# First attention of a two-attention block: its exponentials turned by VectorE and a trip through HBM instead of by TensorE

## The chip, the cores and the metric

The kernel runs on one core of a Trainium2 chip. The metric is the device time of one execution in microseconds (us). A core has five engines that run their own instruction streams and meet at semaphores: TensorE (PE; its weight loads are PEld), VectorE (DVE), ScalarE (ACT), GpSimd (POOL) and SyncE (SP), which here issues every DMA.

## What is computed

For each of 16 samples of 256 channels by 1024 positions, float32:

```python
xn = group_norm(x, 8 groups)                    # then norm_w, norm_b
q, k, v = split(qkv_w @ xn + qkv_b)             # 256 x 1024 each
x = x + proj_w @ (softmax(q.T k / 16) v.T).T + proj_b
t = tokens(x)                                   # 1024 x 256
u = layer_norm(t);  n = u / |u|
t = t + softmax((n n.T) ** 2) u
y = sign(w - mean(w)) * mean(|w|) applied to layer_norm(t), + bias
t = t + round(7 * clip(y, -1, 1)) / 7
out = tokens back to channels
```

Both softmaxes are over rows of 1024. Products are made of float32 values cut into a high and a low float32r part, three matmuls in the place of one (low x high, high x low, high x high), so each operand of a product exists twice, as `_hi` and `_lo`.

## The kernel before

One sample follows the other, software-pipelined by hand: `front(b, f)` does the first attention of sample b and the scores of the second, together with the feed-forward layer of the sample before (f = b - 1), and `back(b)` does the eight products of the second attention. The order of every engine's work is written out by hand in its block's `front` and `back`, and 14 of the 16 samples run in a hardware loop.

The first attention goes in eight blocks n of 128 queries. `scores1(b, n)` (PE, L405) writes 128 x 1024 scores into PSUM `wide[n % 2]`, `row_max` (DVE, L889) takes the negative maximum of each row, `exp1` (ACT, L665) writes the exponentials to `expo` in SBUF together with the row sums. The product with v needs the exponentials with keys on the partitions, so `turn_e1` (PE, L429) turns the block by eight 128 x 128 transposes into PSUM `turn`; `e1T_hi` (ACT, L672) rounds it to `eT_hi`, `e1T_lo` (DVE, L894) writes the rest to `eT_lo`, and `product1` (PE, L437) multiplies with v in 24 matmuls of 256 columns. `turn_e1` of block s stands right before `product1` of block s - 1. `residual1` (DVE, L898) divides by the row sum, adds x and takes the moments of the row; POOL makes the coefficients of the layer norm (`layer_norm1`, L1116) and the inverse length of the row (`lengths`, L1119), ACT the normed rows (L678), POOL the unit rows (`unit_rows`, L1132), PE turns these (`turn_cos`, L447), and `cosT_hi`/`cosT_lo` (ACT, DVE) write `tokT_hi` and `tokT_lo`.

The second attention's scores (`scores2`, L455) are computed for the lower triangle alone, in nine parts of growing width; `exp2` (ACT, L698) squares and exponentiates, `e2_hi` (DVE, L916) and `e2_lo` (POOL, L1146) cut the parts, `turn_e2` (PE, L474) and `e2T_parts` (DVE, L927) make the mirrored half. The feed-forward part is `turn_ln2` (PE), `ln2T_hi` (ACT), `ln2T_lo` (DVE), `ffn` (PE, L515), `ffn_out` (ACT), `clip` (DVE), `quantise` (POOL), `turn_t` (PE) and `output` (DVE). `gn_sums`, `group_means`, `gn_deviation`, `group_vars`, `gn_variance` belong to the next sample's group norm.

## Time and profile before

| | us |
|---|---|
| three runs, median | 1856.28 (1855.66 to 1859.16) |
| the profiled execution's own time | 1856.45 |
| its span | 1854.7 |
| TensorE busy | 1835.7 (99%) |
| VectorE, GpSimd, ScalarE busy | 1268.1 (68%), 959.6 (52%), 906.7 (49%) |
| DMA, mean over the span | 19 GB/s |

The span is the time from the first to the last instruction in the profile; 1.75 us lie around it. TensorE's granted clock is 0.998 of full speed on average.

### The profile page before, as it was taken

The numbers are of one execution on the slowest core, as the hardware profiler recorded it, in microseconds if no ns is written. First come the engines' busy times: TensorE is split into PE (matmuls) and PEld (weight loads), VectorE is DVE, ScalarE is ACT, GpSimd is POOL, SyncE is SP. The second block draws the span as 40 slices with busy tenths as digits, with TensorE's granted clock in tenths as the row PEclk, the third lists the DMA queues.
The fourth block names the chain that finished last, engine by engine and source line by source line (L and its number), as shares of the span: only waits on it lengthen the run. The fifth ranks groups of instructions, "written<-read, shape, count | busy, mean of one in ns | idle before, by whom it ended". The sixth has DMA issues, their size and how long they took to land.

```text
span 1854.7 us, 36871 instructions
## 1 busy us (share of the span) xinstructions
PE 1835.7 (99%) x12834; PEld 1699.1 (92%) x12834; DVE 1268.1 (68%) x2516; ACT 906.7 (49%) x1444; POOL 959.6 (52%) x2262
## 2 busy tenths in 40 slices
PE   7999999999999999999999999999999999999997
PEld 6999999989899998999989999999998999989997
DVE  6676766767666676666767667676676766767566
ACT  3545546445463544635446354454544536355452
POOL 0654727457274472734737356372654727447272
PEclk9999999999999999999999999999999999999999
DMA  2000010000100001000010100001000010000000
GB/s 77 1 24 24 1 45 0 23 23 0 45 0 23 23 0 45 0 34 11 0 45 0 45 0 10 35 0 45 0 23 23 0 45 0 23 23 0 24 1 23
DMA packets 16415, 35.42 MB, mean 19 GB/s; under 512 B 2688, under 2 KB 4096, under 8 KB 16384
## 3 DMA queue, kind: packets, MB, share of 16 engines
q1 hardware_dynamic: 16384, 35.01, 5.2%
q8 instruction: 19, 0.31, 0.1%
q14 instruction: 12, 0.10, 0.0%
HBM read 18.23 MB, written 16.78 MB: 19 GB/s over the span
## 4 chain that ended last, share of the span: by engine, by line
PE 98%; DVE 0%; DMA 0%; ACT 0%; SPq 0%; issue 0%; POOL 0%; ACTq 0%; POOLq 0%; DVEq 0%
PE wide L322 35%; PE narrow L424 8%; PE narrow L426 8%; PE narrow L425 8%; PE turn L434 6%; PE wide L424 5%; PE wide L426 5%; PE wide L425 5%; PE narrow L322 5%; PE wide L520 3%; PE turn L481 3%; PE turn L377 2%; PE narrow L452 2%; PE turn L511 1%; PE turn L528 1%; DMA qkv_b_c<-in_L_conv_qkv_b 0%
## 5 line engine op out<-in xcount | busy, mean ns | idle before, releaser
L322 PE MATMUL wide<-xn_hi,prob 128*128 128x512 f32 x1024 | 310.1, 404 | 0.0
L676 ACT ACTIVATE prob<-turn 128x1024 fp32r<-128x1024 f32 x128 | 131.3, 1026 | 322.0 <-PE turn L434 322.0
L1109 POOL TENSOR_TENSOR ln_v<-ln_mv,ln_eps 128x1 f32<-128x1 f32 x256 | 49.3, 193 | 428.8 <-DVE ln_mv L909 251.7
L891 DVE TENSOR_REDUCE neg_max<-wide 128x1 f32<-128x1024 f32 x128 | 156.4, 1222 | 123.0 <-PE wide L322 123.0
L690 ACT ACTIVATE ln<-tok,ln_shift,ln_r 128x256 f32<-128x256 f32 x128 | 77.2, 603 | 319.7 <-POOL ln_shift L1114 319.7
L424 PE MATMUL narrow<-prob 128*128 128x256 f32 x768 | 225.0, 293 | 0.0
L426 PE MATMUL narrow<-prob 128*128 128x256 f32 x768 | 217.0, 283 | 0.0
L425 PE MATMUL narrow<-prob 128*128 128x256 f32 x768 | 216.9, 282 | 0.0
L322 PEld LDWEIGHTS wide<-xn_hi,prob 128*128 128x128 f32 x1024 | 182.8, 188 | 35.4
L896 DVE TENSOR_TENSOR prob<-turn,prob 128x1024 fp32r<-128x1024 f32 x128 | 156.7, 1224 | 61.8 <-ACT prob L676 61.8
L669 ACT ACTIVATE expo<-wide,neg_max 128x1024 f32<-128x1024 f32 x128 | 142.5, 1113 | 58.2 <-DVE neg_max L891 58.1
L322 PE MATMUL wide<-xn_lo,prob 128*128 128x512 f32 x512 | 160.7, 395 | 0.0
L1149 POOL TENSOR_TENSOR prob<-expo,prob 128x128 fp32r<-128x128 f32 (+6 forms) x112 | 150.3, 1358 | 9.0 <-DVE prob L919 9.0
L424 PE MATMUL narrow<-val,prob 128*128 128x258 f32 x512 | 148.6, 290 | 0.0
L425 PEld LDWEIGHTS narrow<-prob 128*128 128x128 f32 x768 | 147.1, 191 | 0.0
L424 PE MATMUL wide<-val,prob 128*128 128x258 f32 x512 | 146.9, 287 | 0.0
L424 PEld LDWEIGHTS narrow<-prob 128*128 128x128 f32 x768 | 146.9, 191 | 0.0
L426 PEld LDWEIGHTS narrow<-prob 128*128 128x128 f32 x768 | 146.7, 191 | 0.0
L1138 POOL TENSOR_TENSOR cos_x<-ln_x,len_i 128x256 f32<-128x256 f32 x128 | 78.7, 615 | 130.7 <-ACT ln_x L683 126.6
L426 PE MATMUL wide<-val,prob 128*128 128x258 f32 x512 | 145.0, 283 | 0.0
L426 PE MATMUL narrow<-val,prob 128*128 128x258 f32 x512 | 145.0, 283 | 0.0
L425 PE MATMUL wide<-val,prob 128*128 128x256 f32 x512 | 144.6, 282 | 0.0
(171 smaller groups left out, 5479.1 us busy)
## 6 DMA issues: line engine op xcount, KB each, us to landing
x_raw<-in_x SPq DMA_DIRECT2D x32, 512.0 KB, 3.9
out<-y_sb SPq DMA_DIRECT2D x32, 512.0 KB, 2.8
tok<-in_L_conv_qkv_w SPq DMA_DIRECT2D x1, 768.0 KB, 6.8
ln<-in_L_conv_proj_w SPq DMA_DIRECT2D x1, 256.0 KB, 6.8
ln<-in_L_ffn_weight SPq DMA_DIRECT2D x1, 256.0 KB, 3.0
out_bias<-in_L_conv_proj_b SPq DMA_DIRECT2D x1, 128.0 KB, 3.8
qkv_b_c<-in_L_conv_qkv_b SPq DMA_DIRECT2D x1, 3.0 KB, 7.4
norm_w_c<-in_L_conv_norm_w SPq DMA_DIRECT2D x1, 1.0 KB, 6.1
```

What stands on the lines that cost most here:

```text
L322: mm = pe.matmul(o, lhsT, r, start=first and i == 0, stop=last and i == len(parts) - 1)
L424: pe.matmul(o[:, 0:w], hi, value_hi(j), start=j == 0, stop=False)
L425: pe.matmul(o[:, 0:C], hi, value_lo(j), start=False, stop=False, skip_group_check=True)
L426: mm = pe.matmul(o[:, 0:w], lo, value_hi(j), start=False, stop=j == NT - 1)
L434: mm = pe.transpose(turn[:, tile(j)], expo[:, n % DEEP, tile(j)], ident[:, :])
L669: act.activation(expo[:, n % DEEP], wide[n % 2][:, :], ACT.Exp, bias=neg_max[:, n:n + 1], accum_out=row_sum1[:, n:n + 1]).then_inc(e1_made, 1)
L676: act.activation(eT_hi[:, n % 2], turn[:, :], ACT.Copy).then_inc(eT_hi_made, 1)
L690: act.activation(ln2[:, n], tok[:, n], ACT.Identity, bias=ln2_shift[:, n:n + 1], scale=ln2_r[:, n:n + 1]).then_inc(ln2_made, 1)
L891: dve.tensor_reduce(neg_max[:, n:n + 1], wide[n % 2][:, :], AX.X, ALU.max, negate=True).then_inc(max_made, 1)
L896: dve.tensor_sub(eT_lo[:, n % 2], turn[:, :], eT_hi[:, n % 2].bitcast(F32)).then_inc(eT_made, 1)
L1138: pool.tensor_tensor(cos_x[:, r], ln_x[:, r], len_i[:, n:n + 1].broadcast_to([P, C]), ALU.mult).then_inc(cos_made, 1)
L1149: pool.tensor_sub(prob[:, 1, J, row], expo[:, J % DEEP, row], prob[:, 0, J, row].bitcast(F32)).then_inc(p_made, 1)
```

## The change

The eight TensorE transposes of a block of the first attention are taken out. In their place VectorE turns each 32 x 32 square of the block in itself (`e1_turn`), from `expo` into `e_turned` (which is the memory of `x_norm`), SyncE writes the block to a scratch tensor in HBM (`send`, one DMA of 512 KB) and reads it back with the squares at their turned places (`fetch`, four DMAs of 32 partitions, 128 KB each, in runs of 1 KB) into `e_back`. From there `e1T_hi` (ACT) and `e1T_lo` read; `e1T_lo` is on POOL for blocks 0 to 3 and on DVE for 4 to 7. `product1(n)` moves from one block behind the scores to four behind at first: the scores start earlier, between the feed-forward steps of the sample before. Because `x_norm` is lent to the trip, `normalise` moves from the middle of `front` to `back` on ACT. The feed-forward results move from `wide` to `turn`. The row work of the layer norms is grouped: `GROUPS1` cuts the eight blocks into (0,1), (2,3), (4,5), (6), (7) for the first, and three groups serve the second, with one set of POOL coefficient instructions for a group; `unit_rows` goes from POOL to ACT, one instruction per block.

```diff
         a_hi = prob[:, 0, 0:KC, :]
         a_lo = prob[:, 0, KC:2 * KC, :]
         v = prob[:, 0, 2 * KC:2 * KC + NT // 2, :].rearrange("p a (t c) -> p (a t) c", t=2)
-        eT_hi = prob[:, 1, 0:2, :]
-        eT_lo = prob[:, 1, 2:4, :]
+        eT_hi = prob[:, 1, 4:6, :]
+        eT_lo = prob[:, 1, 6:8, :]
+        e_turned = x_norm
+        e_back = sb("e_back", [P, 2, SQ, NT * Q])
+        e_scratch = nc.dram_tensor("e_scratch", (NT, P, N), F32).ap()
+        e_in = e_scratch.rearrange("n (i j) (q f) -> n q j i f", i=SQ, q=SQ)
...
-        out1 = [narrow[0]] * (NT - 2) + [wide[0][:, BANK:N], wide[1][:, BANK:N]]
+        out1 = [narrow[0]] * 4 + [turn[:, 0:BANK], narrow[0], wide[0][:, BANK:N], wide[1][:, BANK:N]]
+        gn_up = turn[:, BANK:BANK + KC]
...
                 load_x(b)
 
+            def send(b, n):
+                sp.wait_ge(e1_turned, NT * b + n + 1)
+                sp.dma_start(e_scratch[n], e_turned[:, n % 2]).then_inc(e1_written[n % 2], 16)
+
+            def fetch(b, n):
+                due = 16 * (HT * b + n // 2 + 1)
+                sp.wait_ge(e1_written[n % 2], due)
+                sp.wait_ge(eT_made[n % 2], due)
+                for q in range(SQ):
+                    sp.dma_start(e_back[q * Q:(q + 1) * Q, n % 2], e_in[n, q]).then_inc(e1_landed[n % 2], 16)
+
+            def front(b, f):
+                send(b, 0)
+                send(b, 1)
+                fetch(b, 0)
+                send(b, 2)
+                fetch(b, 1)
+                send(b, 3)
+                fetch(b, 2)
+                send(b, 4)
...
-            def turn_e1(b, n):
-                pe.wait_ge(e1_made, NT * b + n + 1)
-                if n:
-                    pe.wait_ge(eT_made, NT * b + n)
-                for j in range(NT):
-                    mm = pe.transpose(turn[:, tile(j)], expo[:, n % DEEP, tile(j)], ident[:, :])
-                mm.then_inc(eT_up, 1)
...
             def product1(b, n):
                 if n == 0:
                     pe.wait_ge(v_made, 4 * b + 4)
-                elif n < NT - 2:
+                elif n < 4:
                     pe.wait_ge(t1_made, NT * b + n)
-                pe.wait_ge(eT_made, NT * b + n + 1)
+                elif n == 5:
+                    pe.wait_ge(t1_made, NT * b + 4)
+                pe.wait_ge(eT_made[n % 2], 16 * (HT * b + n // 2 + 2))
                 mm = product(out1[n], lambda j: (eT_hi[:, n % 2, tile(j)], eT_lo[:, n % 2, tile(j)]),
                              lambda j: v[:, j, 0:C], lambda j: v[:, j, C:2 * C])
                 mm.then_inc(pv1_up, 1)
...
+                scores1(b, 0)
+                if f is not None:
+                    pe.wait_ge(xT_made, 2 * b + 2)
+                    turn_ln2(f, 0)
+                scores1(b, 1)
                 values(b, 2)
                 values(b, 3)
                 if f is not None:
-                    pe.wait_ge(a_made, 2 * b + 2)
+                    ffn(f, 0)
+                scores1(b, 2)
+                if f is not None:
+                    pe.wait_ge(y_made, 4 * f + 2)
+                    turn_ln2(f, 1)
+                scores1(b, 3)
+                if f is not None:
                     ffn(f, 1)
+                scores1(b, 4)
+                if f is not None:
+                    pe.wait_ge(y_made, 4 * f + 4)
                     turn_t(f, 0)
-                    pe.wait_ge(y_made, 4 * f + 2)
-                scores1(b, 0)
+                product1(b, 0)
+                scores1(b, 5)
                 if f is not None:
                     pe.wait_ge(out_made, 2 * f + 1)
                     turn_t(f, 1)
-                    pe.wait_ge(y_made, 4 * f + 4)
-                scores1(b, 1)
+                product1(b, 1)
+                scores1(b, 6)
+                product1(b, 2)
...
+                if more:
+                    group_means(b + 1)
+                scores1(b, 7)
+                turn_cos(b, 0)
+                if more:
+                    group_vars(b + 1)
+                product1(b, 3)
+                scores2(b, 0)
+                scores2(b, 1)
+                product1(b, 4)
+                product1(b, 5)
+                turn_cos(b, 1)
+                product1(b, 6)
...
+                    pe.wait_ge(gn_var, b + 2)
+                turn_e2(b, 1)
+                scores2(b, 2)
+                scores2(b, 3)
+                turn_cos(b, 2)
+                product1(b, 7)
+                turn_e2(b, 2)
+                scores2(b, 4)
+                turn_e2(b, 3)
+                turn_cos(b, 3)
+                scores2(b, 5)
+                turn_e2(b, 4)
+                scores2(b, 6)
+                turn_e2(b, 5)
+                turn_cos(b, 4)
+                scores2(b, 7)
+                scores2(b, 8)
+                turn_e2(b, 6)
...
             def e1T_hi(b, n):
-                act.wait_ge(eT_up, NT * b + n + 1)
+                act.wait_ge(e1_landed[n % 2], 16 * SQ * (HT * b + n // 2 + 1))
                 if n >= 2:
                     act.wait_ge(pv1_up, NT * b + n - 1)
-                act.activation(eT_hi[:, n % 2], turn[:, :], ACT.Copy).then_inc(eT_hi_made, 1)
...
+                e1T_hi(b, 0)
+                exp1(b, 3)
+                if f is not None:
                     ffn_out(f, 1, reuse)
...
+                e1T_hi(b, 1)
+                exp1(b, 4)
+                e1T_hi(b, 2)
+                exp1(b, 5)
+                e1T_hi(b, 3)
+                layer_norm1(b, 0)
+                exp1(b, 6)
+                unit_rows(b, 0)
+                e1T_hi(b, 4)
+                exp1(b, 7)
+                cosT_hi(b, 0)
...
+                layer_norm1(b, 2)
+                exp2(b, 2)
+                unit_rows(b, 2)
+                exp2(b, 3)
+                cosT_hi(b, 2)
+                layer_norm1(b, 3)
+                unit_rows(b, 3)
+                exp2(b, 4)
+                cosT_hi(b, 3)
+                layer_norm1(b, 4)
+                unit_rows(b, 4)
+                exp2(b, 5)
+                exp2(b, 6)
+                cosT_hi(b, 4)
+                exp2(b, 7)
+                exp2(b, 8)
...
+            def e1_turn(b, n):
+                dve.wait_ge(e1_made, NT * b + n + 1)
+                if n >= 2:
+                    dve.wait_ge(e1_written[n % 2], 16 * (HT * b + n // 2))
+                dve.transpose(e_turned[:, n % 2].rearrange("p (q n t) -> p n q t", q=SQ, n=NT),
+                              expo[:, n % DEEP].rearrange("p (n q t) -> p n q t", q=SQ, n=NT)).then_inc(e1_turned, 1)
+
             def e1T_lo(b, n):
                 dve.wait_ge(eT_hi_made, NT * b + n + 1)
-                dve.tensor_sub(eT_lo[:, n % 2], turn[:, :], eT_hi[:, n % 2].bitcast(F32)).then_inc(eT_made, 1)
+                dve.tensor_sub(eT_lo[:, n % 2].rearrange("p (n i t) -> p n i t", n=NT, i=SQ),
+                               e_back[:, n % 2].rearrange("p i (n t) -> p n i t", n=NT),
+                               eT_hi[:, n % 2].rearrange("p (n i t) -> p n i t", n=NT, i=SQ).bitcast(F32)
+                               ).then_inc(eT_made[n % 2], 16)
...
+                row_max(b, 6)
+                e1_turn(b, 6)
+                residual1(b, 2)
+                if more:
+                    gn_deviation(b + 1)
+                e1T_lo(b, 4)
+                row_max(b, 7)
+                cosT_lo(b, 0)
+                e1_turn(b, 7)
+                if more:
+                    gn_variance(b + 1)
+                residual1(b, 3)
+                e1T_lo(b, 5)
+                e2_hi(b, 0)
...
+                residual1(b, 7)
+                e2T_parts(b, 2)
+                e2_hi(b, 4)
+                cosT_lo(b, 3)
+                e2T_parts(b, 3)
+                e2_hi(b, 5)
+                e2T_parts(b, 4)
+                cosT_lo(b, 4)
+                e2_hi(b, 6)
+                e2T_parts(b, 5)
+                e2_hi(b, 7)
+                e2_last_lo(b, 7)
+                e2T_parts(b, 6)
+                e2_hi(b, 8)
+                e2_last_lo(b, 8)
...
+            def e1T_lo(b, n):
+                pool.wait_ge(eT_hi_made, NT * b + n + 1)
+                pool.tensor_sub(eT_lo[:, n % 2].rearrange("p (n i t) -> p n i t", n=NT, i=SQ),
+                                e_back[:, n % 2].rearrange("p i (n t) -> p n i t", n=NT),
+                                eT_hi[:, n % 2].rearrange("p (n i t) -> p n i t", n=NT, i=SQ).bitcast(F32)
+                                ).then_inc(eT_made[n % 2], 16)
...
             def front(b, f, more):
                 if f is not None:
                     quantise(f, 0)
+                e1T_lo(b, 0)
+                e1T_lo(b, 1)
+                if f is not None:
                     quantise(f, 1)
-                for n in range(NT - 1):
-                    layer_norm1(b, n)
-                    lengths(b, n)
-                    unit_rows(b, n)
-                    value_lo(b, n)
```

The functions `layer_norm1`, `lengths`, `value_lo`, `turn_cos`, `cosT_hi` and `cosT_lo` take a group g in the place of a block n and work on all of its blocks.

**Where the order moves, first place.** ScalarE, from the first feed-forward output to the second exponential blocks, before (`tokT_hi<-turn` is `ln2T_hi`, `y_sb` is `ffn_out`, `prob<-narrow` is `value_hi`, `expo,row_sum1` is `exp1`, `prob<-turn` is `e1T_hi`):

```order
L712 ACTIVATE tokT_hi<-turn 128x2x512 [waits ln2T_up]
L721 ACTIVATE y_sb<-wide0,ffn_b_c,w_mean 128x512 [waits y_up]
L721 ACTIVATE y_sb<-wide0,ffn_b_c,w_mean 128x512
L661 ACTIVATE prob<-narrow0 128x2x256 [waits v_up]
L661 ACTIVATE prob<-narrow1 128x2x256 [waits v_up]
L721 ACTIVATE y_sb<-wide1,ffn_b_c,w_mean 128x512 [waits y_up]
L721 ACTIVATE y_sb<-wide1,ffn_b_c,w_mean 128x512
L669 ACTIVATE expo,row_sum1<-wide0,neg_max 128x1024 [waits max_made]
L676 ACTIVATE prob<-turn 128x1024 [waits eT_up]
L669 ACTIVATE expo,row_sum1<-wide1,neg_max 128x1024 [waits max_made]
L676 ACTIVATE prob<-turn 128x1024 [waits eT_up]
```

and now, from the same feed-forward output:

```order
L796 ACTIVATE y_sb<-turn,ffn_b_c,w_mean 128x512 [waits y_up]
L796 ACTIVATE y_sb<-turn,ffn_b_c,w_mean 128x512
L727 ACTIVATE expo,row_sum1<-wide0,neg_max 128x1024 [waits max_made]
L787 ACTIVATE tokT_hi<-turn 128x2x512 [waits ln2T_up]
L734 ACTIVATE prob<-e_back 128x1024 [waits e1_landed0]
L727 ACTIVATE expo,row_sum1<-wide1,neg_max 128x1024 [waits max_made]
L796 ACTIVATE y_sb<-turn,ffn_b_c,w_mean 128x512 [waits y_up]
L796 ACTIVATE y_sb<-turn,ffn_b_c,w_mean 128x512
```

The second `ln2T_hi` stood ahead of the first feed-forward output and of all exponentials; now it stands behind the third exponential, and the second `ffn_out` behind the fourth.

**Second place.** ScalarE around the last exponential of the first attention, before (`ln_x` and `val` are `layer_norm1`, `x_norm` is `normalise`, `tokT_hi<-narrow1` is `cosT_hi`):

```order
L645 ACTIVATE x_norm<-x_raw,gn_b,gn_a 128x1024 [waits gn_scale]
L695 ACTIVATE tokT_hi<-narrow1 128x2x128 [waits cosT_up]
L676 ACTIVATE prob<-turn 128x1024 [waits pv1_up,eT_up]
L669 ACTIVATE expo,row_sum1<-wide1,neg_max 128x1024 [waits eT_up,max_made]
L683 ACTIVATE ln_x<-tok,ln_shift,ln_r 128x256 [waits val_made,ln1_scale]
L686 ACTIVATE val<-ln_x 128x256 [waits ln1_made]
L695 ACTIVATE tokT_hi<-narrow1 128x2x128 [waits cosT_up]
L676 ACTIVATE prob<-turn 128x1024 [waits pv1_up,eT_up]
```

and now (`cos_x` is `unit_rows`, `prob<-e_back` is `e1T_hi`):

```order
L727 ACTIVATE expo,row_sum1<-wide0,neg_max 128x1024 [waits e1_turned,max_made]
L756 ACTIVATE cos_x<-ln_x,len_i 128x256 [waits len_steps]
L756 ACTIVATE cos_x<-ln_x,len_i 128x256
L734 ACTIVATE prob<-e_back 128x1024 [waits pv1_up,e1_landed0]
L727 ACTIVATE expo,row_sum1<-wide1,neg_max 128x1024 [waits e1_turned,max_made]
L768 ACTIVATE tokT_hi<-narrow1 128x2x256 [waits cosT_up]
L734 ACTIVATE prob<-e_back 128x1024 [waits pv1_up,e1_landed1]
```

Three `cosT_hi` of a sample stood ahead of its last exponential (the third is the second row shown); now the first of them is the instruction right behind that exponential.

**Third place.** VectorE in the second attention, before (`prob<-expo` is `e2_hi`, `prob<-turn` is `e2T_parts`, `tokT_lo` is `cosT_lo`):

```order
L919 CAST prob<-expo 128x512 [waits e2_made]
L930 CAST prob<-turn 128x3x128 [waits pT_up]
L932 TENSOR_TENSOR prob<-turn,prob 128x3x128 [waits pT_hi_made]
L913 TENSOR_TENSOR tokT_lo<-narrow1,tokT_hi 128x2x128 [waits cosT_hi_made]
L919 CAST prob<-expo 128x640 [waits e2_made]
L930 CAST prob<-turn 128x4x128 [waits pT_up]
L932 TENSOR_TENSOR prob<-turn,prob 128x4x128 [waits pT_hi_made]
L919 CAST prob<-expo 128x768 [waits e2_made]
L913 TENSOR_TENSOR tokT_lo<-narrow1,tokT_hi 128x2x128 [waits cosT_hi_made]
L930 CAST prob<-turn 128x5x128 [waits pT_up]
L932 TENSOR_TENSOR prob<-turn,prob 128x5x128 [waits pT_hi_made]
L919 CAST prob<-expo 128x896 [waits e2_made]
```

and now:

```order
L1023 CAST prob<-expo 128x640 [waits e2_made]
L1017 TENSOR_TENSOR tokT_lo<-narrow1,tokT_hi 128x2x128 [waits cosT_hi_made]
L1034 CAST prob<-turn 128x3x128 [waits pT_up]
L1036 TENSOR_TENSOR prob<-turn,prob 128x3x128 [waits pT_hi_made]
L1023 CAST prob<-expo 128x768 [waits e2_made]
L1034 CAST prob<-turn 128x4x128 [waits pT_up]
L1036 TENSOR_TENSOR prob<-turn,prob 128x4x128 [waits pT_hi_made]
L1017 TENSOR_TENSOR tokT_lo<-narrow1,tokT_hi 128x2x128 [waits cosT_hi_made]
L1023 CAST prob<-expo 128x896 [waits e2_made]
L1034 CAST prob<-turn 128x5x128 [waits pT_up]
```

The turned halves of block 4 (`128x4x128`) stood ahead of the cast of block 5 (`128x768`); now they stand behind it. The last `cosT_lo` stood ahead of the halves of block 5 and now too, but it belongs to a `turn_cos` that TensorE issues right before the scores that need it.

## Rows read from the trace of the kernel before

**Rows 1.** Page, part 1: busy us (share) xinstructions

```profile
PE 1835.7 (99%) x12834; PEld 1699.1 (92%) x12834; DVE 1268.1 (68%) x2516; ACT 906.7 (49%) x1444; POOL 959.6 (52%) x2262
```

**Rows 2.** TensorE's waits: who waited for whom, us, times, longest

```profile
PE narrow L364 <- DVE gn_mv L856: 7.3, 1, 7.3
```

**Rows 3.** Chain of waits in order of time: start us, us, what

```profile
949.80 0.87 PE turn L434 x8
...
954.36 0.12 PE narrow L424
...
957.23 2.81 PE wide L322 x12
...
1000.84 1.39 PE wide L322 x6
...
1006.88 0.44 PE turn L481 x4
...
1007.54 2.47 PE wide L322 x12
```

**Rows 4.** Groups by line: busy us, mean ns | idle before

```profile
L896 DVE TENSOR_TENSOR prob<-turn,prob 128x1024 fp32r<-128x1024 f32 x128 | 156.7, 1224 | 61.8 <-ACT prob L676 61.8
...
L712 ACT ACTIVATE tokT_hi<-turn 128x1024 fp32r<-128x1024 f32 x31 | 31.7, 1021 | 33.0 <-PE turn L511 33.0
...
L695 ACT ACTIVATE tokT_hi<-narrow 128x256 fp32r<-128x256 f32 x128 | 47.9, 374 | 18.0 <-PE narrow L452 16.9
...
L913 DVE TENSOR_TENSOR tokT_lo<-narrow,tokT_hi 128x256 fp32r<-128x256 f32 x128 | 52.5, 410 | 21.9 <-ACT tokT_hi L695 21.9
...
L683 ACT ACTIVATE ln_x<-tok,ln_shift,ln_r 128x256 f32<-128x256 f32 x128 | 76.6, 599 | 10.5 <-POOL ln_shift L1114 10.5
```

**Rows 5.** Timeline, one sample of the loop: start us, us, engine, line, operation

```profile
945.96 1.03 PE L528 MATMUL turn<-ident,tok 128*128 128x128 f32 x8
...
946.16 1.23 DVE L891 TENSOR_REDUCE neg_max<-wide 128x1 f32<-128x1024 f32 x1 [0.36 <-PE wide L322]
...
947.42 1.12 ACT L669 ACTIVATE expo<-wide,neg_max 128x1024 f32<-128x1024 f32 x1 [3.48 <-DVE neg_max L891]
...
948.43 0.19 ACT L669 ACTIVATION_READ_ACCUMULATOR expo<-wide,neg_max 128x1 f32 x1
```

**Rows 6.** Timeline, VectorE between the score blocks

```profile
963.94 0.16 DVE L861 COPY gn_m<-narrow 128x2 f32<-128x2 f32 x1 [0.71 <-PE narrow L364]
...
965.06 0.16 DVE L867 TENSOR_TENSOR gn_e<-gn_e,gn_mv 128x2 f32<-128x2 f32 x1
...
984.30 0.17 DVE L902 RECIPROCAL inv_sum<-row_sum 128x1 f32<-128x1 f32 x1 [0.58 <-PE narrow L426]
...
985.51 0.06 DVE L804 MEMSET carrier<- 128x1 f32 x1
```

**Rows 7.** Timeline, ScalarE and VectorE in the second attention

```profile
1007.05 0.81 ACT L706 ACTIVATE expo<-wide 128x768 f32<-128x768 f32 x1 [0.50 <-PE wide L322]
...
1007.49 0.68 DVE L930 CAST prob<-turn 128x512 fp32r<-128x512 f32 x1
...
1007.90 0.85 ACT L708 ACTIVATE expo<-expo 128x768 f32<-128x768 f32 x1
...
1008.81 0.93 DVE L919 CAST prob<-expo 128x768 fp32r<-128x768 f32 x1
```

**Rows 8.** Groups by line, GpSimd and VectorE

```profile
L1104 POOL TENSOR_TENSOR xn_lo<-x_norm,xn_hi 128x1024 fp32r<-128x1024 f32 x30 | 80.7, 2709 | 0.0
...
L924 DVE TENSOR_TENSOR prob<-expo,prob 128x512 fp32r<-128x512 f32 x32 | 82.1, 2567 | 1.1
```

**Rows 9.** Page, part 6: DMA issues, KB each, us to landing

```profile
x_raw<-in_x SPq DMA_DIRECT2D x32, 512.0 KB, 3.9
...
out<-y_sb SPq DMA_DIRECT2D x32, 512.0 KB, 2.8
```

**Rows 10.** Windows at the end: us, busy of each engine, PEclk, DMA

```profile
1845.00:1850.00 5.00, 3.06 (x12) 2.36 (x10) 3.02 (x4) 1.45 (x2) 0.00 (x0) 0.72 0.27 105
```

More of the change, by code:

```diff
@@ L36 @@
 BANK = 512
+Q = 32
 GROUPS = 8
@@ L731, in front @@
                 if f is not None:
-                    ln2T_hi(f, 1)
-                    ffn_out(f, 0, reuse)
+                    ln2T_hi(f, 0)
+                exp1(b, 0)
+                exp1(b, 1)
                 value_hi(b, 2)
@@ L755, in front @@
-                cosT_hi(b, 5)
-                for u in range(2, NP):
-                    J = PARTS[u][0]
-                    if J in (4, 6):
-                        cosT_hi(b, J // 2 + 4)
-                    exp2(b, u)
-                    if J == 3:
-                        layer_norm1(b, NT - 1)
+                    ffn_out(f, 0, reuse)
+                exp1(b, 2)
+                if f is not None:
+                    ln2T_hi(f, 1)
+                e1T_hi(b, 0)
+                exp1(b, 3)
@@ L984, in front @@
                 value_lo(b, 1)
+                row_max(b, 0)
+                if f is not None:
+                    ln2T_lo(f, 0)
+                e1_turn(b, 0)
+                row_max(b, 1)
+                value_lo(b, 2)
+                e1_turn(b, 1)
+                value_lo(b, 3)
+                if f is not None:
+                    clip(f, 0)
+                row_max(b, 2)
                 if f is not None:
                     ln2T_lo(f, 1)
-                    clip(f, 0)
-                value_lo(b, 2)
@@ L989, in front @@
-                value_lo(b, 3)
+                e1_turn(b, 2)
+                row_max(b, 3)
+                e1_turn(b, 3)
                 if f is not None:
                     clip(f, 1)
+                row_max(b, 4)
+                if f is not None:
                     output(f, 0)
-                row_max(b, 0)
+                e1_turn(b, 4)
+                residual1(b, 0)
+                if more:
+                    gn_sums(b + 1, 0)
+                row_max(b, 5)
                 if f is not None:
@@ L995, in front @@
                     output(f, 1)
-                row_max(b, 1)
-                e1T_lo(b, 0)
+                e1_turn(b, 5)
+                residual1(b, 1)
                 if more:
-                    gn_sums(b + 1, 0)
-                for s in range(1, NT + 1):
-                    if more and s == 3:
-                        gn_deviation(b + 1)
-                    if s >= 2:
-                        residual1(b, s - 2)
-                    if s + 1 < NT:
-                        row_max(b, s + 1)
-                    if more and s == 3:
-                        gn_variance(b + 1)
-                    if s >= 4:
-                        cosT_lo(b, s - 4)
-                    if s < NT:
-                        e1T_lo(b, s)
-                    if more and s == 1:
-                        gn_sums(b + 1, 1)
@@ L1015, in front @@
[L1015 to L1029 removed]
+                    gn_sums(b + 1, 1)
@@ new lines, in front @@
+                e1T_lo(b, 6)
+                residual1(b, 5)
+                cosT_lo(b, 1)
+                e1T_lo(b, 7)
+                residual1(b, 6)
+                e2T_parts(b, 1)
+                e2_hi(b, 2)
+                e2_hi(b, 3)
+                cosT_lo(b, 2)
+                residual1(b, 7)
[5 more added lines that the diff above has]
+                e2T_parts(b, 4)
```

339 lines of the change are left out of this document (170 added, 169 removed).

## The prediction

> **What bounds the kernel now.** I read the busy times first: TensorE works 1835.7 of 1854.7 us, the others half to two thirds of the span [rows 1]. Then its waits: the longest is 7.3 us, once, at the start [rows 2]; in the loop there are none. So each microsecond taken from TensorE is one taken from the time, as long as nobody makes it wait in its place. The chain in order of time is TensorE's program and gives serial prices [rows 3]: the eight transposes of `turn_e1` 0.87 us, a `scores1` 2.81, a `product1` 2.87 (954.36 to 957.23), the scores of part 3 1.39, of part 6 2.47, `turn_e2(4)` 0.44.
>
> **What goes.** 16 samples x 8 blocks x 0.87 = 111.4 us. The profiled execution took 1856.45 us (span 1854.7 and 1.75 around it; the median of the three runs is 1856.28), so without one new wait the time would be 1745.1. The break-even is 111.4 / 16 = 6.96 us of TensorE waiting per sample.
>
> **Where TensorE would wait.** The other engines work in order, so what counts is where each row stands in its queue. I walked through one sample with prices from rows: a row-wide tensor operation on DVE 1.22 [rows 4], a `row_max` 1.23 and, 0.2 behind the end of a TensorE group; `exp1` 1.12 and 0.19 for its sums, 1.20 until the next engine may start; a hand-over between DVE and ACT 0.03 [rows 5]. The VectorE turn is nowhere in this trace. It moves 1024 elements per partition, as the rows at 1.22 do, so 1.22 is the nearest and what I take; below, 0.7 as for 512 columns [rows 7], if two elements moved at a time; above, twice the row, 2.45.
>
> A. `ffn(1)` behind `scores1(3)`. The second `ln2T_hi` now stands behind `exp1(2)` on ACT (first place of the order). From the end of `scores1(2)`: 0.20 + 1.23 + 0.03 + 1.12 + 1.02 [rows 4] + 1.22 for `ln2T_lo` = 4.8. TensorE has `turn_ln2(1)` and `scores1(3)` in that time, 0.87 + 2.81 = 3.7. Wait 1.15.
>
> B. `turn_t(0)` wants the second `ffn_out`, which stands behind `exp1(3)`; DVE comes to that row's maximum only after `ln2T_lo` and `e1_turn(2)`. Wait 0.2.
>
> C. `group_vars` wants `gn_deviation`. On DVE it stands behind `e1_turn(6)` (1.22) and `residual1(2)` (984.30 to 985.57: 1.3), and takes 1.3 itself (963.94 to 965.22) [rows 6]; the turn can't start before `exp1(6)`, which on ACT stands behind the first pair of layer norms and ends about 0.35 after `product1(2)`. That makes 0.35 + 3.7 = 4.05 from the product's end; TensorE comes there at 0.12 + 2.81 + 0.4 = 3.35. Wait 0.7.
>
> D. `scores2(0)` wants the first `cosT_lo`. Ahead of it stand `e1T_lo(4)`, `row_max(7)`, `exp1(7)` and `cosT_hi(0)` (second place). From the same product's end: `row_max(7)` starts at 5.2, then 1.23 + 1.20 + 0.6 + 0.7 for the two halves of 512 columns (they lie between the 256 and the 1024 columns of [rows 4]), 9.0. TensorE, C included, is there at 4.1 + 0.1 + 2.87 = 7.1. Wait 1.7 to 1.9; I take 1.7. Were DVE free for `row_max(7)` at once, 0.5 would stay.
>
> E. `turn_cos(1)` behind `product1(5)`: its unit rows stand on ACT behind the layer norms of blocks 2, 3 and `e1T_hi(6)`, all of it hanging on `residual1(3)`, which D has made late. 0.7, and 0.2 more before `product1(6)`. 0.9.
>
> F. `turn_cos(2)` behind `scores2(3)`: from the end of part 2, 0.2 + two passes over 384 columns, 1.05, + two scalings of 256 columns, 1.1 [rows 4] = 2.35; TensorE has 1.39. Wait 0.95.
>
> G. `turn_e2(5)` wants the turned halves of block 4, which now stand behind the cast of block 5 (third place). From the end of `scores2(5)`: ACT is free at 0.7 (a layer norm and its unit row stand first), then 0.81 + 0.85, cast 0.93, halves 0.68 and 0.7 [rows 7] = 4.7. TensorE has 0.44 + 2.47 = 2.9. Wait 1.75; with ACT free and the cast at 0.5, 0.9.
>
> H. `turn_cos(4)` stands right before the `scores2(7)` that needs it: 0.2 + 0.37 + 0.41 [rows 4] after the transposes. Wait 1.0. Before, a block of scores lay between.
>
> The sum is 1.15 + 0.2 + 0.7 + 1.7 + 0.9 + 0.95 + 1.75 + 1.0 = 8.35 us per sample, x 16 = 133.6. The first sample has no feed-forward part and so neither A nor B, but its `product1(0)` comes so soon behind the scores that it waits some 3 us for the trip; I count it like the others. 1745.1 + 133.6 = 1878.7, so **1879 us**.
>
> **What is hidden.** The trip: a store of 512 KB lands in 2.8 us, a load in 3.9 [rows 9]; four issues for one make it some 4.4, so 7.2 both ways. By my walk (us from the sample's start): `fetch(n)` is queued on SP behind `send(n + 1)` or further, so block 0, turned at 17.5 us of the sample, is back at 27.2, rounded at 28.7, its low part at 31.4 (2.7 on POOL [rows 8]), and `product1(0)` starts at 34.7: 3.3 to spare. Blocks 1, 2, 3 have 2.4, 2.8, 2.3. With ACT in order, a trip longer by 2 us would first hold up `exp1(3)` and `exp1(4)`. Blocks 5 and 6 have 0.7 and nothing. The ACT and POOL instructions that were regrouped stand beside TensorE's work; POOL loses the unit rows, and ACT's eight scalings of 0.6 are in E, F and G. `normalise` in `back` has 24 us of `product2` over it.
>
> A row speaks against `e1T_lo`: a DVE subtraction of 512 columns with both inputs in SBUF, while POOL works, takes 2.57 us, where 1024 columns with one input in PSUM take 1.22 [rows 8, 4]. The new `e1T_lo` has both in SBUF, on DVE for blocks 4 to 7, with POOL busy. Between 1.22 and 1.22 + 2.7 (a whole POOL subtraction first); I take 1.22 but for block 6, where 0.5 more is in E. At its worst blocks 5 and 6 come 2.7 late, 2 us per sample beyond their slack, and the time is 1878.7 + 32 = 1911. The Trainium skill (SBUF — State Buffer, "Who interferes with whom") says that a VectorE instruction with two SBUF inputs and a GpSimd one that uses SBUF exclude each other for a whole instruction; by that rule the 1911 would be the sum, by the row of 1.22 it is 1879.
>
> **Rivals.**
> 1. *The side engines keep up, and the change is faster.* For: they idle a third to half of the time [rows 1], and B, C, E hang on queues in which I may have put an instruction too early. Against: A, F, G, H are chains within the sample that start at TensorE itself. With B, C, E at nothing, D 0.5, G 0.9: 4.5 per sample, 1745.1 + 72 = 1817; halfway 1840. The change is faster from under 6.96 us of waits per sample on.
> 2. *The turn takes twice a pass, 2.45.* B, C (and D behind it) and E each grow by 1.2: 3.6 x 16 = 58, 1937. Against: nothing in the trace.
> 3. *Products wait*, for the ports (above) or for the trip: 1 to 2 us in two products per sample, 1911 to 1940.
> 4. *The clock falls.* At the end of this trace TensorE works 3.06 of 5 us with some 1.9 of idle time between, and its granted clock there is 0.72 of full speed, from 1.0 [rows 10]: that is its 2.4 GHz level left for its 1.2 GHz level part of the time. G and H leave it 0.7 us of work in 3.5. If the 3.4 us of matmuls behind them ran at 1.2 GHz, that is 3.4 x 16 = 55 more, 1934. Against: none of my gaps is as long as that one. The Trainium skill (TensorE: Matmul & The Clock Gate, "Part 1: The HAM clock gate") calls this a gate that an idle engine closes; by it this rival would hold if G and H count as idle, and else not.
>
> **How the numbers follow.** Forecast (waits of 7.2 to 10 per sample, 1860 to 1905) 0.45; rival 1 0.30; rival 2 0.08; rival 3 0.09; rival 4 0.08. A measurement of this kernel tells 0.2% (3.7 us) from no change. Within it lie waits of 6.7 to 7.2 per sample, an edge of the forecast and of rival 1: 0.05. Faster 0.28, slower 0.67. The forecast's own range is 1860 to 1905; the range that leaves out 2 in 10 goes from rival 1's floor, 1818, to above rivals 2 and 4, 1942.
>
> **What would show it.** In the changed profile: `turn_e1` gone and TensorE's busy time near 1725 us; its waits, by total: `ffn` <- `ln2T_lo`, `scores2` <- `cosT_lo` (D and H), `turn_cos` <- unit rows of ACT, `turn_e2` <- `e2T_parts`, each once or twice per sample and 16 to 28 us in all; the turn at 1.2 us; no product's wait over 0.5 us per sample; PEclk 1.0. Wrong it would be if `turn_e2` and `turn_cos` don't wait, if the turn costs 2 us, or if a DMA stands in TensorE's or ACT's longest waits.

## The result, and the profile after

The changed kernel takes 1975.79 us (median of four, 1972.13 to 1978.41) against 1855.97 for the kernel before: a ratio of 1.0641, 95% interval 1.0628 to 1.0654. It is 6.4% slower. The direction was forecast; the size was not, and 1976 lies 34 us above the range's end of 1942. Two single executions of the experiments lie far outside all others (1993 us for the kernel before, beside x5 to x8, and 3584 us for x8) and are left out of their ratios.

The page of the changed kernel, first the line that answers to [rows 1], then the granted clock in 40 slices (tenths of full speed; before all 40 were 9, the highest digit there is):

```profile
PE 1811.1 (92%) x11810; PEld 1638.6 (83%) x11810; DVE 1267.9 (64%) x2532; ACT 936.5 (47%) x1476; POOL 880.2 (45%) x1398
...
PEclk9999999999999989999999999989999899998999
```

TensorE has 1024 instructions less, as it should, but its busy time fell by 24.6 us and not by 111. So there are two losses: waits, and work that got longer. The waits of TensorE (who waited for whom: us, times, longest), against the one line of [rows 2]:

```profile
PE turn L525 <- DVE prob L1036: 39.2, 16, 2.5
PE wide L368 <- DVE tokT_lo L1017: 38.1, 32, 1.6
PE narrow L495 <- ACT cos_x L756: 24.3, 26, 1.6
PE turn L415 <- DVE gn_e L959: 16.6, 16, 1.3
PE turn L564 <- DVE tokT_lo L1054: 15.8, 15, 1.1
PE wide L470 <- DVE prob L995: 9.0, 16, 0.7
PE turn L410 <- DVE gn_mv L948: 7.2, 1, 7.2
PE narrow L470 <- POOL prob L1237: 3.1, 1, 3.1
```

These are G, D with H, E with F, C and A of the prediction, and the wait of `product1(6)`; the two that occur once belong to the first sample. All waits of the list come to 158.7 us; before they came to 12.3. That is 146.4 more.

The second loss. Windows of the changed kernel, from one sample (us; busy and count of PE, PEld, DVE, ACT, POOL; granted clock; DMA share; GB/s):

```profile
1044.00:1048.00 4.00, 2.55 (x22) 2.35 (x21) 2.24 (x3) 2.64 (x4) 0.00 (x0) 1.00 0.49 166
1048.00:1052.00 4.00, 4.00 (x23) 4.00 (x23) 3.15 (x10) 1.39 (x4) 3.14 (x7) 0.57 0.83 260
...
1076.00:1080.00 4.00, 1.67 (x9) 1.34 (x10) 2.40 (x5) 1.34 (x3) 1.94 (x2) 0.90 0.00 0
1080.00:1084.00 4.00, 4.00 (x15) 3.16 (x14) 1.64 (x3) 1.35 (x3) 1.97 (x1) 0.67 0.00 0
```

Twice per sample TensorE is back at work, busy all the time, at a granted clock near half: its 1.2 GHz level in place of 2.4. The timeline of TensorE around both places shows which waits stand ahead (start, us, what; in brackets the idle time before and who ended it):

```profile
1042.64 0.38 PE L415 MATMUL turn<-gn_e,group_mean 128*128 128x2 f32 x2 [0.90 <-DVE gn_e L959]
...
1047.45 0.32 PE L368 MATMUL wide<-tokT_hi,tokT_lo 128*128 128x128 f32 x1 [1.45 <-DVE tokT_lo L1017]
...
1049.28 0.41 PE L470 MATMUL turn<-prob 128*128 128x256 f32 x1
...
1052.11 0.28 PE L472 MATMUL turn<-prob 128*128 128x256 f32 x1
```

```profile
1077.40 0.76 PE L525 MATMUL turn<-ident,expo 128*128 128x128 f32 x5 [2.47 <-DVE prob L1036]
1077.99 0.38 PE L495 MATMUL narrow<-ident,cos_x 128*128 128x128 f32 x2
1079.31 0.80 PE L368 MATMUL wide<-tokT_hi,tokT_lo 128*128 128x512 f32 x1 [0.93 <-DVE tokT_lo L1017]
1079.90 0.63 PE L368 MATMUL wide<-tokT_lo,tokT_hi 128*128 128x512 f32 x1
```

A `product1` matmul takes 0.41 us behind the first pair of waits (C and D) and 0.28 three microseconds later; a score matmul over 512 columns takes 0.63 behind the second pair (G and H), and 0.40 elsewhere. No wait of these four is longer than 2.5 us.

This sample doesn't stand for all. In 15 samples the second fall stands behind G and H. The first stands behind C and D in 6 of them only; in the other 9 the clock holds there and falls some 10 us later, behind the two waits of E (`turn_cos(1)` and `product1(6)`). One of the nine:

```profile
560.06 0.32 PE L368 MATMUL wide<-tokT_hi,tokT_lo 128*128 128x128 f32 x1 [1.45 <-DVE tokT_lo L1017]
560.22 0.28 PE L368 MATMUL wide<-tokT_lo,tokT_hi 128*128 128x128 f32 x1
...
568.54 0.63 PE L495 MATMUL narrow<-ident,cos_x 128*128 128x128 f32 x4 [1.08 <-ACT cos_x L756]
569.82 0.39 PE L470 MATMUL wide<-prob 128*128 128x256 f32 x1 [0.65 <-DVE prob L995]
...
571.08 0.41 PE L472 MATMUL wide<-prob 128*128 128x256 f32 x1
```

Over the span, in windows of 2 us, the granted clock is down at 33 places, each of which costs up to 1.7 or 3.4 us; before there were 2, both at the end of the program. The mean granted clock is 0.962; before it was 0.998. Of 1976.3 us that takes at most (1 - 0.962) x 1976.3 = 75 us, before it took at most 4. TensorE was busy in 135 of the 150 us at the lower level, which makes 68.

The book then nearly closes: 1854.7 - 111.4 + 146.4 + 71 = 1960.7, and the span is 1976.3. The 16 left (21 with the 68) would be 0.13 us for each of the 121 waits that are new. That they belong to the waits isn't shown by a run of its own; the rows above show only that the first matmul behind a wait takes 0.32 to 0.39 us, where later ones of the kind take 0.28 and overlap, one every 0.12 us.

### The profile page after: what moved, and what is told of

It reads as the page before. It is cut to its first block, busy times and chain, and to the rows that moved or that the text cites. A ratio compares the mean times of both kernels' runs of the same rounds, so it can differ in the third digit from the quotient of the medians.

```text
span 1976.3 us, 34635 instructions
## 1 busy us (share of the span) xinstructions
PE 1811.1 (92%) x11810; PEld 1638.6 (83%) x11810; DVE 1267.9 (64%) x2532; ACT 936.5 (47%) x1476; POOL 880.2 (45%) x1398
## 4 chain that ended last, share of the span: by engine, by line
PE 46%; POOL 23%; issue 14%; DVE 5%; ACT 5%; DMA 3%; SPq 2%; POOLq 1%; ACTq 0%; DVEq 0%
PE wide L368 16%; POOL prob L1237 5%; PE narrow L368 4%; PE wide L470 3%; PE wide L472 3%; PE wide L471 3%; PE narrow L470 3%; PE narrow L472 3%; PE narrow L471 3%; DMA e_back<-e_scratch 3%; POOL val L1276 3%; POOL ln_r L1250 2%; POOL sq_root L1264 2%; PE turn L525 2%; POOL prob L1282 2%
## 5 line engine op out<-in xcount | busy, mean ns | idle before, releaser
L1237 POOL TENSOR_TENSOR prob<-e_back,prob 128x1024 fp32r<-128x1024 f32 x64 | 153.5, 2399 | 162.4 <-ACT prob L734 161.3
L990 DVE STREAM_TRANSPOSE x_norm<-expo 128x1024 f32<-128x1024 f32 x128 | 158.7, 1240 | 79.0 <-ACT expo L727 77.0
L470 PE MATMUL narrow<-prob 128*128 128x256 f32 x640 | 185.8, 290 | 3.1 <-POOL prob L1237 3.1
L471 PE MATMUL narrow<-prob 128*128 128x256 f32 x640 | 182.0, 284 | 0.0
L472 PE MATMUL narrow<-prob 128*128 128x256 f32 x640 | 181.9, 284 | 0.0
L1282 POOL TENSOR_TENSOR prob<-expo,prob 128x128 fp32r<-128x128 f32 (+6 forms) x112 | 159.5, 1424 | 46.6 <-DVE prob L1023 46.6
L734 ACT ACTIVATE prob<-e_back 128x1024 fp32r<-128x1024 f32 x128 | 135.0, 1055 | 78.9 <-DMA e_back<-e_scratch 78.3
L368 PE MATMUL wide<-tokT_hi,tokT_lo 128*128 128x512 f32 (+3 forms) x384 | 137.2, 398 | 38.1 <-DVE tokT_lo L1017 38.1
L1247 POOL TENSOR_TENSOR ln_v<-ln_mv,ln_eps 128x2 f32<-128x2 f32 (+2 forms) x128 | 26.7, 208 | 318.4 <-DVE ln_mv L1049 244.8
L781 ACT ACTIVATE expo<-wide 128x128 f32<-128x128 f32 (+2 forms) x144 | 85.3, 593 | 142.4 <-PE wide L368 140.9
L1292 POOL TENSOR_TENSOR carrier_p<-ones 128x1 f32<-128x1 f32 x60 | 11.7, 195 | 316.0 <-DVE y_sb L1059 313.5
L1023 DVE CAST prob<-expo 128x128 fp32r<-128x128 f32 (+2 forms) x144 | 80.4, 567 | 111.0 <-ACT expo L783 111.0
```

The source lines that it names most:

```text
L368: mm = pe.matmul(o, lhsT, r, start=first and i == 0, stop=last and i == len(parts) - 1)
L470: pe.matmul(o[:, 0:w], hi, value_hi(j), start=j == 0, stop=False)
L471: pe.matmul(o[:, 0:C], hi, value_lo(j), start=False, stop=False, skip_group_check=True)
L472: mm = pe.matmul(o[:, 0:w], lo, value_hi(j), start=False, stop=j == NT - 1)
L734: act.activation(eT_hi[:, n % 2].rearrange("p (n i t) -> p n i t", n=NT, i=SQ), e_back[:, n % 2].rearrange("p i (n t) -> p n i t", n=NT), ...
L781: act.activation(e, wide[J % 2][:, offset(J) + c0:offset(J) + c1], ACT.Square).then_inc(sq2_made, 1)
```

## The experiments

Two theories went into them. A: the loss is the waits at the places that the walk named, plus a clock that falls behind gaps close together. B: the longer matmuls have another cause (the DMA traffic, the SBUF rows). Later a third, C: the waits aren't the order's, and move on when one is taken away. All runs stand beside runs of the kernel before (1855.8 to 1857.0). "Rest" is the span, less waits, less unread matmuls, less the 1731.0 that before has without waits (1842.4) and without the transposes (111.4).

| run | us (median) | waits | clock | falls | (1 - clock) x span | rest |
|---|---|---|---|---|---|---|
| changed kernel | 1975.8 | 158.7 | 0.962 | 33 | 75 | 87 |
| x1 fillers, 40 | 1993.1 | 128.4 | 0.983 | 18 | 34 | 47 |
| x5 fillers, 24 | 1933.9 | 80.9 | 0.996 | 3 | 8 | 20 |
| x2 swap at G | 1922.4 | 137.4 | 0.984 | 18 | 31 | 49 |
| x3 swap at D | 1944.9 | 156.2 | 0.981 | 17 | 37 | 53 |
| x4 five places | 1890.8 | 114.6 | 0.988 | 11 | 23 | 42 |
| x6 x4 and three more | 1878.1 | 103.2 | 0.987 | 13 | 24 | 40 |
| x8 x6 and fillers, 7 | 1860.2 | 78.3 | 0.997 | 3 | 6 | 18 |
| x9 x6 and three others | 1893.1 | 121.3 | 0.991 | 10 | 17 | 38 |
| x10 x9 and fillers, 2 | 1893.2 | 110.6 | 0.988 | 13 | 23 | 38 |
| x11 x9, GpSimd's order | 1897.4 | 113.3 | 0.983 | 17 | 32 | 49 |
| x12 x11 without G's swap | 1929.3 | 141.4 | 0.974 | 19 | 50 | 55 |
| x7 turn at 2.45 | 2077.6 | 233.7 | 0.953 | 42 | 98 | 116 |

All but the first column are of the profiled execution. The clock's column is an upper bound, as TensorE is idle in part of the time at the lower level. The rest follows it in every row, 5 to 21 us above it.

**Fillers.** They make nothing earlier. In x5, beside x1 (the waits that keep these PSUM parts free are left out):

```
+def busy(o, n):
+    for _ in range(n):
+        pe.matmul(o, sign_w[:, 0, 0:P], sign_w[:, :, :], start=True, stop=True)
 product1(b, 3)
+busy(wide[0][:, 0:BANK], 5)       # x1: 10 of 256 columns
 scores2(b, 0)
...
 product1(b, 5)
+busy(wide[0][:, BANK:N], 4)       # x1: none
 turn_cos(b, 1)
...
+busy(narrow[0][:, :], 3)          # x1: 6 of 256
 turn_cos(b, 2)
...
 scores2(b, 6)
+busy(narrow[0][:, :], 9)          # x1: 18 of 256
 turn_e2(b, 5)
 turn_cos(b, 4)
+busy(narrow[0][:, :], 3)          # x1: 6 of 256
 scores2(b, 7)
```

x1: 

> The changed kernel with small matmuls that nobody reads (128x256, 0.12 us apart) put where TensorE waits: 10 before scores2(0), 18 before turn_e2(5), 6 before turn_cos(2), 6 before scores2(7). They are shorter than or as long as the waits there, so no wait goes and nothing gets earlier. Theory A (the gaps make the granted clock fall, and the work behind them at the lower level is what my sum lacked): granted clock back to 0.99 or more, the slow matmuls behind the gaps gone, 1976 - 60 to 80 = 1895 to 1915 us. Rival B (the longer matmuls come from something else, the DMA trip or the two-input VectorE rows): clock and time as they are, 1976 or, where a filler is longer than its wait, up to 1985.

Measured 1993.1 us, clock 0.983. Wrong in the sum, but 15 of the 33 falls were gone. Two things ate it: the falls that are left (9 behind `turn_cos(1)`, which had no filler, and 6 beside the stall), and a stall at the head of the loop that stands in no other kernel's list of TensorE's waits. The first line of x1's:

```profile
PE narrow L470 <- issue: 36.8, 12, 4.0
```

x5: 

> As the first filler kernel, but with 24 unread matmuls of 512 columns (0.23 us apart) in place of 40 of 256: 5 before scores2(0), 4 before turn_cos(1), 3 before turn_cos(2), 9 before turn_e2(5), 3 before scores2(7). The first one removed the clock falls behind scores2(0) and turn_e2(5), but had a new one behind turn_cos(1) and a stall of 2 to 4 us without a releaser at the head of the loop. Theory A: with turn_cos(1) filled too no fall is left, the clock is 0.99 or more, and without that stall 1976 - 70 = 1895 to 1915 us; with the stall (12 times some 3 us) 1935 to 1950. Rival B (the lower clock isn't the gaps' doing): no change, or more.

Measured 1933.9 us, clock 0.996: 42 us faster than the changed kernel, with 384 matmuls more. The stall did not come back. The unread matmuls were busy for 102.9 us while the waits gave up 77.8, so they cost 25, and the rest fell from 87 to 20. That is the cause shown: with the gaps filled, and every other engine's program as it was, 67 us go. Theory B can't do that.

**One swap each.**

```
# x2, VectorE
 e2T_parts(b, 3)
-e2_hi(b, 5)
 e2T_parts(b, 4)
+e2_hi(b, 5)
# x3, ScalarE
+cosT_hi(b, 0)
 exp1(b, 7)
-cosT_hi(b, 0)
```

x2: 

> The changed kernel with one pair swapped on VectorE: the turned halves of block 4 (e2T_parts) ahead of the cast of block 5. Theory A: the wait of turn_e2(5) goes (2.45 us, 16 times: 39 us) and with it the second clock fall of a sample (1.7 us lost, 27 us): 1976 - 66 = 1910. Without the clock in it: 1937. Rival C (the wait is not the order's, it turns up one step later): above 1960.

Measured 1922.4: 53 us gained. The wait went (39.2 to 0) and 15 falls with it, but the wait behind `cosT_lo` grew from 38.1 to 56.4 us: TensorE now comes to H sooner than the `cosT_lo` that it needs, and waits 2.09 us there in place of 0.93.

x3: 

> The changed kernel with one pair swapped on ScalarE: the first cosT_hi ahead of exp1(7). Theory A: the wait of scores2(0) goes (about 1.45 us x 16 = 23) and with it the first clock fall of a sample (27 us), as the gap of 0.9 at group_vars then stands alone: 1976 - 50 = 1926. Without the clock: 1953. Rival C (scores2(0) then waits for exp1(7) or a low part just the same): above 1965.

Measured 1944.9: 31 us gained. D's wait went (38.1 to 14.9, which is H's) and 16 falls, and `turn_cos` waits 42.0 in place of 24.3. Of the first falls of a sample only three are left, at E, and none stands behind C, which waits 1.1 us alone now. Both swaps pay less than forecast (66 and 50 us) but more than the waits they remove (21 and 3 us in the sum of all waits): the rest goes with the clock's column (44 and 38 us less).

**All five places** (D, G; H: `turn_cos(4)` ahead of `turn_e2(5)` and `cosT_hi(4)` ahead of the third `exp2` from the end; A: second `ln2T_hi` ahead of `exp1(2)`; C: `group_means` and `gn_deviation` ahead of `product1(2)` and `residual1(2)`).

x4: 

> The changed kernel with five places of the orders altered: e2T_parts(4) ahead of the cast of block 5, first cosT_hi ahead of exp1(7), turn_cos(4) ahead of turn_e2(5) and its cosT_hi ahead of exp2(6), second ln2T_hi ahead of exp1(2), group_means and gn_deviation ahead of product1(2) and residual1(2). Theory A: waits A, C, D, G, H of the prediction (16 + 17 + 23 + 39 + 15 = 110 us) and both clock falls go; left are turn_cos behind unit rows (24), the products' low parts (12) and the start (10): 1745 + 46 = 1790 to 1810, faster than before. Rival C (the side engines have no slack, waits move on): 1860 to 1930.

Measured 1890.8 us: 85 us gained where 165 to 185 were expected, so theory C holds for half of it. A is gone from the list, C became a wait of the same size at `group_means`, and D's gain turned up at `turn_cos(1)`, whose unit rows wait for GpSimd. Behind its wait of 1.77 us and the product's of 0.63 stand 8 of the 11 falls that are left.

**Three more:** `group_means` back, `residual1(3)` ahead of `e1_turn(7)` on VectorE, `gn_coefficients` behind the second `lengths` on GpSimd.

x6: 

> The order kernel before with three more edits: group_means back behind product1(2) with only gn_deviation ahead of residual1(2); residual1(3) ahead of e1_turn(7) on VectorE; gn_coefficients behind the second group's lengths on GpSimd. Theory A: the waits at group_means (19 us) and at turn_cos(1) (1.77 x 16 = 28, to under 10) go, and with the latter the last clock fall (27 us); 1890 - 19 - 20 - 27 = 1825 us, faster than before. Rival C (the side engines have no slack, waits move on): 1860 to 1890.

Measured 1878.1 us. The wait of `turn_cos(1)` went from 1.77 us to nothing, and that of `turn_cos(2)` grew to 2.85, with the clock's fall behind it in ten samples of sixteen (windows of x6, one of the ten):

```profile
1006.00:1010.00 4.00, 1.15 (x8) 0.74 (x7) 2.29 (x7) 3.90 (x9) 3.75 (x8) 1.00 0.00 0
1010.00:1014.00 4.00, 4.00 (x23) 4.00 (x22) 1.12 (x2) 2.35 (x5) 3.61 (x9) 0.57 0.00 0
```

x8 (four unread matmuls ahead of `turn_cos(1)` and three ahead of `turn_cos(2)`): 

> The order kernel with the three more edits and seven unread matmuls of 512 columns per sample, 4 before turn_cos(1) and 3 before turn_cos(2). Theory A: if the edits alone leave a clock fall behind these two places, this takes it away: 15 to 30 us under the kernel without fillers. If they leave none: the same, or up to 10 us slower, as the fillers are then longer than the waits.

Measured 1860.2 us, ratio to the kernel before 1.0019 (1.0009 to 1.0030). Seven matmuls that compute nothing make it 18 us faster. It is the best of all the versions and still no faster than the kernel before.

**What GpSimd makes late.**

x9 (`unit_rows(2)` ahead of `exp2(2)`; the coefficients and lengths of blocks 4 and 5 ahead of `value_lo(1)`, `e2_lo(1)` and `gn_coefficients`; `gn_deviation` ahead of `e1_turn(6)`): 

> The order kernel with the three more edits (1878 us, of which turn_cos(2) waits 2.85 us once a sample, 42 us in all, and one clock fall stands behind it), and three edits that shorten what turn_cos(2) and group_vars wait for: on GpSimd the second-group low parts and gn_coefficients behind the lengths of blocks 4 and 5, on ScalarE unit_rows(2) ahead of exp2(2), on VectorE gn_deviation ahead of e1_turn(6). Theory A: the wait of turn_cos(2) falls from 2.85 to 0.8 us (33 us) and the clock fall goes (some 27 us), group_vars saves 10: 1878 - 70 = 1808 us, clock 0.99 or more, faster than before. Rival C (waits move on): 1850 to 1878. The floor is 1745 plus what is left of waits.

x10 (x9 and two fillers): 

> The same with two unread matmuls of 512 columns ahead of turn_cos(2). Theory A: no clock fall is left to take away, so this costs nothing to 8 us (32 x 0.23); if a fall is still there, 20 us less than without them.

x11 (x9 with `gn_deviation` back, and block 6's coefficients and lengths ahead of `e2_lo(1)` too): 

> The order kernel with the three more edits (1878 us), unit_rows(2) ahead of exp2(2) on ScalarE, and on GpSimd the coefficients and lengths of blocks 4 and 5 and then of block 6 ahead of e2_lo(1), the low parts of group 2 and gn_coefficients; gn_deviation stays behind e1_turn(6). In the kernel of 1893 us product1(3) waited 1.38 us behind that deviation and turn_cos(3) 1.46 us, as GpSimd came to block 6 4.6 us after its rows. Theory A: both go, and the chain behind turn_cos(3) (exp2(5), turn_e2(5), scores2(7)) gets earlier: 1893 - 10 - 23 - 15 = 1845 us, clock 0.99 or more, faster than before. Rival C (waits move on): 1870 to 1890.

Measured 1893.1, 1893.2 and 1897.4, each 15 to 19 us slower than x6. The sums of x9 and x11 are wrong, each beyond its rival's range too. x10's fillers cost nothing, as its theory A said, but not for its reason: falls were left, 10 in x9 and 13 in x10. In both kernels most of them stand behind `scores2(7)`, where x10 has no filler. In x9 `turn_cos(2)` waits 0.79 in place of 2.85, and the 2 us come back as 1.38 at `product1(3)`, 1.46 at `turn_cos(3)` and 1.23 at `scores2(7)`. In x11 (timeline, TensorE) the chain behind `turn_cos(4)`, H's edit, stands bare:

```profile
1029.89 0.41 PE L495 MATMUL narrow<-ident,cos_x 128*128 128x128 f32 x2 [1.13 <-ACT cos_x L756]
...
1031.37 0.77 PE L525 MATMUL turn<-ident,expo 128*128 128x128 f32 x5 [1.07 <-ACT expo L783]
...
1033.34 0.79 PE L368 MATMUL wide<-tokT_hi,tokT_lo 128*128 128x512 f32 x1 [1.20 <-DVE tokT_lo L1017]
```

From a block's residual to its unit rows it takes four and five tiny GpSimd operations in a row, 4.5 us (x6: 994.55 to 999.0), and this chain runs four times between the last score block and `product2`. My reading is that with the transposes gone there is less of TensorE's work to lie over the chain than it is long, and that a wait ahead of it had hidden its later parts. It is read from these three traces and not shown: no run shortened the chain.

**One gap in a kernel of short ones.**

x12: 

> The kernel run beside it, with the one pair on VectorE (cast of block 5, turned halves of block 4) back in the order of the changed kernel, so that turn_e2(5) waits about 2.5 us again, the other waits being short. If one gap of 2.5 us is enough for a clock fall: 2.5 + some 1.7 us per sample, 60 to 70 us over the kernel beside it, clock about 0.985. If the falls need gaps close together: 40 us, clock as beside it.

Measured 1929.3 us, 32 over x11, clock 0.974 against 0.983. Neither case: x11 has a fall of its own at this place in nearly every sample (three gaps of 1.1 to 1.2 us close together), and in x12 the gap is 4.10 us, not 2.5; the clock falls inside it, while TensorE does nothing (windows of x12):

```profile
1044.00:1048.00 4.00, 1.65 (x8) 0.96 (x7) 0.17 (x1) 3.07 (x7) 3.77 (x7) 1.00 0.00 0
1048.00:1052.00 4.00, 1.13 (x6) 1.13 (x7) 3.76 (x5) 1.83 (x3) 2.94 (x3) 0.62 0.00 0
1052.00:1056.00 4.00, 4.00 (x11) 3.13 (x11) 1.65 (x2) 1.04 (x2) 1.98 (x1) 0.52 0.00 0
```

**The dearer turn.** An unread reduction of 1.2 us ahead of each turn on VectorE:

```
+dve.tensor_reduce(unread[:, n:n + 1], expo[:, n % DEEP], AX.X, ALU.max)
 dve.transpose(e_turned[:, n % 2]..., expo[:, n % DEEP]...)
```

x7: 

> The changed kernel with an unread row-wide reduction (1.2 us) on VectorE ahead of each e1_turn, so that the turn costs 2.45 us as rival 2 of the prediction supposed. By the walk of the prediction waits B, C, D and E grow by 1.2 each: 3.6 to 4.8 us per sample, 1976 + 58 to 77 = 2034 to 2053; with the clock falling longer behind them up to 2080. If VectorE had slack in this stretch: under 2000.

Measured 2077.6 us, 102 more: the waits grew by 75.0 us (4.7 per sample) and the clock's share by 23. The sum is the upper end of the walk, but it came together by luck. C grew by 1.5 per sample and B appeared. A, which the walk left alone, more than doubled (15.8 to 33.8 us), products came to wait for a block's residual, 24 us that stood in no list, and D with H fell from 38.1 to 20.0. Lines of x7:

```profile
PE turn L416 <- DVE gn_e L960: 40.5, 16, 2.7
PE turn L565 <- DVE tokT_lo L1056: 33.8, 15, 2.3
PE narrow L471 <- DVE tok L1008: 24.3, 17, 1.6
PE wide L369 <- DVE tokT_lo L1019: 20.0, 19, 2.2
PE turn L573 <- ACT y_sb L797: 13.5, 13, 1.1
```

## Why the prediction was wrong

Step by step, by TensorE's waits in the changed profile, per sample:

| | predicted | measured |
|---|---|---|
| A `ffn(1)` | 1.15 | 1.05 (15.8 / 15) |
| B `turn_t(0)` | 0.2 | none |
| C `group_vars` | 0.7 | 1.04 |
| D and H, `cosT_lo` | 2.7 | 2.38 |
| E and F, unit rows | 1.65 | 1.52 |
| E, `product1(6)` | 0.2 | 0.56 |
| G `turn_e2(5)` | 1.75 | 2.45 |
| in all (measured: 146.4 / 16, with the start) | 8.35 | 9.15 |

**Right.** All the places but B, and their sum within 10%; the first sample's product waits 3.1 us, where some 3 were foreseen. G is 0.7 short, and that is the cast of block 5, which took 1.63 us and not 0.93. The turn costs 1.24 us (predicted 1.22), so rival 2 falls. The trip lands in 3.0 and 3.2 us. None of TensorE's waits is put down to its DMAs, so rival 3 falls but for 12 us of low parts. But one sign of being wrong did show: a DMA stands fifth among ACT's waits, 78.3 us in all. In the sample of 1010 to 1060 us ACT waits so at blocks 0 to 3 (0.27 to 1.92 us), and no product waits behind it. No run made the trip shorter, so what it passes on stays unmeasured.

```profile
ACT prob L734 <- DMA e_back<-e_scratch: 78.3, 54, 3.5
...
L990 DVE STREAM_TRANSPOSE x_norm<-expo 128x1024 f32<-128x1024 f32 x128 | 158.7, 1240 | 79.0 <-ACT expo L727 77.0
...
e_scratch<-x_norm SPq DMA_DIRECT2D x128, 512.0 KB, 3.0
e_back<-e_scratch SPq DMA_DIRECT2D x512, 128.0 KB, 3.2
```

**Wrong.** The step that failed is rival 4: "Against: none of my gaps is as long as that one", with a chance of 0.08. The clock fell behind 0.90 and 1.45 us, behind 1.08 and 0.65, and behind 2.47 and 0.93. The row that I measured them against [rows 10] was misread: it lies behind that fall, not ahead of it. In the five microseconds before it the granted clock is 0.94 already, and the wait ahead of the lower clock is one of 2.41 us (kernel before, windows and timeline):

```profile
1840.00:1845.00 5.00, 2.59 (x14) 2.02 (x15) 3.38 (x5) 2.15 (x3) 0.00 (x0) 0.94 0.00 0
```

```profile
1843.46 0.50 PE L520 MATMUL narrow<-tokT_lo,sign_w 128*128 128x512 f32 x1 [2.41 <-DVE tokT_lo L950]
1843.79 0.39 PE L520 MATMUL narrow<-tokT_hi,sign_w 128*128 128x512 f32 x1
```

G alone measured longer than that (2.47, where I had 1.75), and waits shorter than it were enough where two stood close together. I priced the rival at 55 us, 3.4 in each sample behind H; two places in each sample cost 71 at most. The rest of the miss is two smaller terms: the waits were 13 us longer in all than my 133.6, and the 16 us of the book, which I had at nothing. The walk's sum with the measured waits and no clock would be 1745.1 + 146.4 + 16 = 1908, 3 us above the forecast's own range; with the clock it is 1979. The Trainium skill (TensorE: Matmul & The Clock Gate, "Part 1: The HAM clock gate") calls this a gate that an idle engine closes, and the trace agrees with that much: 33 falls with the gaps, 3 with the gaps filled. Ahead of the first fall shown TensorE had worked 2.55 of 4 us.

The range failed with it. I treated the rivals as cases that exclude each other, each added to the same sum. A fall of the clock is no rival to waits: it is what waits do, and its price belonged in the forecast's own sum.

Left open: why the same waits bring a fall in some samples and not in others. E's pair had one in 9 samples of the changed kernel at 1.08 and 0.65 us, and in 3 of x3 at 1.7 and 0.63. Left open too: where the 37 us of stall at the loop's head in x1 came from. Its loop has 40 unread matmuls more per sample; x5 has 24 more, before has 64 more than the changed kernel, and neither stalls. And no run undid the grouped row work or the move of `unit_rows` to ScalarE, so what these two give or take is not known.
